# Transposing one of two expert tiles on VectorE instead of TensorE in a fused conditional-mixing and mixture-of-LoRA kernel

## What is computed

```python
# x: (128, 64, 1024) f32, cond_128: (128, 128)
h = gelu(embedding @ W0 + b0); h = gelu(h @ W1 + b1)
att = softmax(h @ W2 + b2)                              # (128, 8)
agg_w = einsum('bk,koi->boi', att, weight[..., 0])      # a 64x64 channel mix for each sample
agg_b = att @ bias_k
y = einsum('boi,bih->boh', agg_w, x) + agg_b[:, :, None]
y = y.reshape(-1, 1024)                                 # 8192 rows
probs = softmax(y @ W_router.T)                         # 8 experts
topk_probs, topk_idx = top_k(probs, 2); topk_probs /= sum(topk_probs)
combine = the two weights put at their experts          # (8192, 8)
h = einsum('nd,erd->ner', y, A)                         # 8 experts x rank 16 = 128 columns
hw = h * combine[:, :, None]                            # the weighted activations
out = x + y @ W_base.T + b_base + einsum('ner,eor->no', hw, B) * 2
```

## Time and profile before

| | before |
|---|---|
| median of 3 runs | 954.34 us (954.16 to 954.8) |
| the profiled execution, its own time | 954.3 us |
| its span, first to last instruction | 952.6 us |
| granted TensorE clock | 1.00 in all 40 slices |
| PE busy | 945.1 us (99%) |
| DVE busy | 695.5 us (73%) |
| ACT busy | 332.8 us (35%) |
| POOL busy | 89.1 us (9%) |
| HBM traffic over the span | 117 GB/s |

### The profile page before, as it was taken

The page is one execution under the profiler, slowest core; times in us unless marked ns, Lnnn a source line. Parts: engine busy times, 40 slices in busy tenths (PEclk is TensorE's granted clock), DMA queues, the critical chain, the costliest instruction groups (busy, mean ns, idle before and its releaser), DMA issues.

```text
span 952.6 us, 18810 instructions
## 1 busy us (share of the span) xinstructions
PE 945.1 (99%) x6745; PEld 940.2 (99%) x6745; DVE 695.5 (73%) x1554; ACT 332.8 (35%) x671; POOL 89.1 (9%) x134
## 2 busy tenths in 40 slices
PE   9999999999999999999999999999999999999997
PEld 8999999999999999999999999999999999999997
DVE  4889776768776768777777777777777677767686
ACT  5653332333332333332333333333333333323431
POOL 0011010101010100100100100010101010101010
PEclk9999999999999999999999999999999999999999
DMA  8434444343444354435353434344434344444434
GB/s 304 140 75 132 110 119 132 92 132 91 111 115 133 90 134 91 111 113 130 94 133 92 112 113 119 105 118 105 114 113 109 115 108 104 120 118 104 120 90 111
DMA packets 35233, 111.33 MB, mean 117 GB/s; under 512 B 13040, under 2 KB 13424, under 8 KB 30864
## 3 DMA queue, kind: packets, MB, share of 16 engines
q1 hardware_dynamic: 25712, 76.36, 21.9%
q0 software_dynamic: 9216, 33.56, 21.2%
q10 hardware_dynamic: 288, 1.19, 0.4%
HBM read 75.37 MB, written 35.65 MB: 117 GB/s over the span
## 4 chain that ended last, share of the span: by engine, by line
PE 97%; DMA 1%; DVE 1%; issue 0%; ACT 0%; DVEq 0%; ACTq 0%
PE ps L416 25%; PE ps L420 25%; PE ps L418 25%; PE ps L476 9%; PE ps L452 4%; PE ps L450 4%; PE ps L454 4%; DMA w_stage<-in_wide 1%; PE ps L499 1%; PE ps L442 0%; PE ps L443 0%; PE ps L502 0%; PE ps L513 0%; DVE sum L931 0%; DVE x_sb L1220 0%
## 5 line engine op out<-in xcount | busy, mean ns | idle before, releaser
L416 PE MATMUL ps<-w_hi,x_hi 128*128 128x290 f32 x1544 | 460.3, 298 | 0.3 <-DVE sum L931 0.3
L418 PE MATMUL ps<-w_lo,x_hi 128*128 128x290 f32 x1544 | 457.7, 296 | 0.0
L420 PE MATMUL ps<-w_hi,x_lo 128*128 128x290 f32 x1544 | 456.9, 296 | 0.0
L416 PEld LDWEIGHTS ps<-w_hi,x_hi 128*128 128x128 f32 x1544 | 291.5, 189 | 2.5 <-issue 1.5
L420 PEld LDWEIGHTS ps<-w_hi,x_lo 128*128 128x128 f32 x1544 | 291.3, 189 | 0.0
L418 PEld LDWEIGHTS ps<-w_lo,x_hi 128*128 128x128 f32 x1544 | 291.2, 189 | 0.0
L684 ACT CAST x_hi<-xT_sb 128x512 fp32r<-128x512 f32 x186 | 115.6, 621 | 190.9 <-DVE xT_sb L928 163.4
L912 DVE TENSOR_TENSOR x_lo<-xT_sb,x_hi 128x512 fp32r<-128x512 f32 x186 | 127.4, 686 | 34.3 <-ACT x_hi L684 34.3
L889 POOL DMA_DIRECT2D x_sb<-in_x x64 | 56.4, 881 | 512.0 <-DVE x_sb L1002 512.0
L988 DVE TENSOR_TENSOR hwT_lo<-ps,hwT_hi 128x128 fp32r<-128x128 f32 x64 | 18.7, 291 | 97.7 <-ACT hwT_hi L696 96.9
L699 ACT COPY sum<-ps 128x580 f32<-128x580 f32 x96 | 61.9, 645 | 62.9 <-PE ps L420 62.1
(11 more groups left out here) (123 smaller groups left out, 1127.6 us busy)
## 6 DMA issues: line engine op xcount, KB each, us to landing
x_sb<-in_x POOLq DMA_DIRECT2D x64, 512.0 KB, 5.4
result<-x_sb SPq DMA_DIRECT2D x63, 512.0 KB, 2.8
xT_sb<-in_xT SPq DMA_DIRECT2D x31, 1024.0 KB, 4.8
b_sb<-in_wide SPq DMA_DIRECT2D x2, 1160.0 KB, 14.7
agg_w_rows<-agg_w SPq DMA_DIRECT2D x1, 2048.0 KB, 7.5
mix<-agg_w_rows SPq DMA_DIRECT2D x124, 16.0 KB, 2.5
w_stage<-in_wide ACTq DMA_DIRECT2D x2, 580.0 KB, 8.0
w_stage<-in_wide SPq DMA_DIRECT2D x2, 580.0 KB, 11.5
```

Source lines behind the costliest of these rows:

```text
L416: nc.tensor.matmul(dst, x_hi[:, s, rows], high[:, c, cols], start=first, stop=False, skip_group_check=True)
L418: nc.tensor.matmul(dst, x_hi[:, s, rows], low[:, c, cols], start=False, stop=False, skip_group_check=True)
L420: mm = nc.tensor.matmul(dst, x_lo[:, s, rows], high[:, c, cols], start=False, stop=last, skip_group_check=True)
```

## The change

In units 2 to 30 the transpose of the lower tile's hw (tiles 1 to 29 by unit) is taken off TensorE. VectorE does it in 16 STREAM_TRANSPOSE instructions of 32x32, from hw to a new SBUF tile lower_hwT, block (i, j) to block (j, i). Each raises a semaphore, and ScalarE waits for all 16. For this VectorE's route of the lower tile is moved up, ahead of the low part of A22's x (x_low(u, "A22")), and the 16 transposes follow it, also ahead of x_low(u, "A22"). hwT_hi and hwT_lo are then made from lower_hwT in SBUF rather than from PSUM. Unit 1 and the last unit keep TensorE's transpose for both tiles, and so does every unit for its upper tile; the waits of ScalarE for TensorE's transposes are renumbered for it.

```diff
@@ -173,6 +175,7 @@
         bias_out = sb("bias_out", [P, D])
         ar = sb("ar", [P, AR])
         hw = sb("hw", [P, ER])
+        lower_hwT = sb("lower_hwT", [P, P])
         hwT_hi = sb("hwT_hi", [P, P], F32R)
         hwT_lo = sb("hwT_lo", [P, P], F32R)
 
@@ -244,6 +247,7 @@
         ratio_done = sem("ratio_done")
         hw_done = sem("hw_done")
         hwT_mm = sem("hwT_mm")
+        lower_hwT_made = sem("lower_hwT_made")
         hwT_hi_done = sem("hwT_hi_done")
         hwT_lo_done = sem("hwT_lo_done")
         out_mm = sem("out_mm")
@@ -610,7 +614,8 @@
                     pe.wait_ge(w_lo_done, SPLIT_AT["T3"])
                 pe.wait_ge(x_lo_done, splits(u, "S3"))
                 product_part(a, "S3", 0, False)
-                transpose_hw(u - 1, 1)
+                if first:
+                    transpose_hw(u - 1, 1)
                 product_part(a, "S3", 1, False).then_inc(product_mm, 1)
                 experts(u - 1, 1)
                 pe.wait_ge(p5_saved, u)
@@ -691,9 +696,16 @@
                 act.wait_ge(routed, tile_no(u, side) * ROUTE_STEPS + 4)
                 nc.scalar.activation(ratio[:], top_gap[:], ACT.Exp).then_inc(ratio_done, 1)
 
-            def hwT_high(u, side):
-                act.wait_ge(hwT_mm, tile_no(u, side) + 1)
+            def hwT_high(transposes):
+
+                act.wait_ge(hwT_mm, transposes)
                 nc.scalar.copy(hwT_hi[:], hwT).then_inc(hwT_hi_done, 1)
+
+            def lower_hwT_high(u):
+
+                act.wait_ge(lower_hwT_made, u * (BLOCKS * BLOCKS))
+                act.wait_ge(out_mm, tile_no(u, 1))
+                nc.scalar.copy(hwT_hi[:], lower_hwT[:]).then_inc(hwT_hi_done, 1)
 
             def save(dst, first, done):
                 nc.scalar.copy(dst[:], acc(first)).then_inc(done, 1)
@@ -807,7 +819,7 @@
                 act.wait_ge(product_mm, products(u, "A11"))
                 save(sum1, a, p1_saved)
                 x_high("S3")
-                hwT_high(u - 1, 0)
+                hwT_high(1 if first else u + 1)
                 if first:
                     act.wait_ge(t_made, T_AT["T3"])
                     split_weight(T3, t_stage)
@@ -824,7 +836,10 @@
                 gate(u - 1, 1)
                 act.wait_ge(product_mm, products(u, "S1"))
                 save(sum3, b, p5_saved)
-                hwT_high(u - 1, 1)
+                if first:
+                    hwT_high(2)
+                else:
+                    lower_hwT_high(u - 1)
                 z11_high(u)
                 act.wait_ge(xT_in, u * 16 + 16)
                 act.wait_ge(product_mm, products(u, "S3"))
@@ -846,7 +861,7 @@
             act.wait_ge(product_mm, last_products("A11"))
             save(sum1, a, p1_saved)
             x_high("S3")
-            hwT_high(u - 1, 0)
+            hwT_high(LAST + 1)
             act.wait_ge(s_made, sums(u, "S4"))
             act.wait_ge(product_mm, last_products("A12"))
             x_high("S4")
@@ -857,20 +872,20 @@
             mix_high(u, 1)
             gate(u - 1, 1)
             z11_high(u)
-            hwT_high(u - 1, 1)
+            hwT_high(LAST + 2)
             act.wait_ge(product_mm, last_products("S3"))
             save(sum3, a, p5_saved)
             act.wait_ge(product_mm, last_products("A22"))
             nc.scalar.copy(last_hi_left, acc(a)).then_inc(z21_hi_done, 1)
             gate(u, 0)
-            hwT_high(u, 0)
+            hwT_high(LAST + 3)
             act.wait_ge(z22_summed, u + 1)
             nc.scalar.copy(last_hi_right, sum3[:]).then_inc(z22_hi_done, 1)
             for part in range(2):
                 act.wait_ge(last_half_summed, part + 1)
                 nc.scalar.copy(z_hi_right[:, part, :], sum2[:, part, :]).then_inc(last_half_hi_done, 1)
             gate(u, 1)
-            hwT_high(u, 1)
+            hwT_high(LAST + 4)
 
         @block.gpsimd
         def _(pool):
@@ -983,9 +998,17 @@
                     ar[:, lora].rearrange("p (e r) -> p e r", e=EXPERTS), first_w[:, 0:1],
                     expert_w[:].unsqueeze(2).to_broadcast([P, EXPERTS, RANK]), ALU.mult, ALU.mult).then_inc(hw_done, 1)
 
-            def hwT_low(u, side):
+            def transpose_lower(u):
+
+                dve.wait_ge(hw_done, tile_no(u, 1) + 1)
+                for i in range(BLOCKS):
+                    for j in range(BLOCKS):
+                        there, here = slice(j * BLOCK, (j + 1) * BLOCK), slice(i * BLOCK, (i + 1) * BLOCK)
+                        nc.vector.transpose(lower_hwT[there, here], hw[here, there]).then_inc(lower_hwT_made, 1)
+
+            def hwT_low(u, side, whole=hwT):
                 dve.wait_ge(hwT_hi_done, tile_no(u, side) + 1)
-                nc.vector.tensor_tensor(hwT_lo[:], hwT, hwT_hi[:].bitcast(F32), ALU.subtract).then_inc(hwT_lo_done, 1)
+                nc.vector.tensor_tensor(hwT_lo[:], whole, hwT_hi[:].bitcast(F32), ALU.subtract).then_inc(hwT_lo_done, 1)
 
             def result(u, side):
                 t = tile_no(u, side)
@@ -1134,9 +1157,10 @@
                 dve.wait_ge(x_lo_done, splits(u, "A12"))
                 make_s4(u)
                 x_low(u, "S4")
+                route(u - 1, 1)
+                transpose_lower(u - 1)
                 x_low(u, "A22")
-                route(u - 1, 1)
-                hwT_low(u - 1, 1)
+                hwT_low(u - 1, 1, lower_hwT[:])
                 dve.wait_ge(stored[0], u * 16)
                 z11_low(u)
                 put_biases(u, 0)
```

More of the change, by code:

```diff
@@ L80 @@
 GROUPS, GROUP_ROWS = 4, 32
+BLOCK, BLOCKS = 32, 4
 GROUP_COLS = CH * CH // GROUPS
```

## The result

The changed kernel takes 969.32 us (median of 5 runs, 968.18 to 969.53) against 954.58 us before on the same chip: a ratio of 1.0154, 95% interval 1.0142 to 1.0165. It is slower by 1.5%, and the forecast of 951.1 us was wrong in size and in sign. The profiled execution has a span of 967.7 us where before had 952.6, at a clock of 0.999.

A forecast was written before the change was run, and what follows sets the result against it. The prediction took TensorE as the bound, holding 97% of the chain. Only the removed transposes counted, with VectorE's blocks and the move at nothing: 954.34 - 3.28 = 951.06, forecast 951.1 us, range 950.5 to 952.7.

The forecast's parts named there:

- The price of a block: On VectorE, each 32x32 transpose was taken at 0.12 us, from the starts of small steps L973 to L976.
- What it adds on VectorE: VectorE's 16 blocks cost 1.9 us a unit, bounds 0 and 4.6 us, mostly in its idle time before hwT_lo.
- What is moved later: x_low of A22 ends 3.6 us later, delaying SP's xT load; 1.65 us remain before TensorE notices, so no cost.
- The removed transposes: On TensorE, 29 lower-tile transposes at 0.113 us each between matmul starts save 3.28 us, all on the chain.
- rival 1: Blocks from 0.22 us each make xT late and stop PE at mix_upper's z12_lo; 983 us at 0.29 us; chance 6%.
- The upper bound of 0.29 us: Highest price per VectorE block, from the 128-column subtraction L988 if nothing overlaps.
- The threshold: Blocks may cost 0.22 us each before the late xT load, via make_s1 and z12_low, stops TensorE.
- The move costed at nothing: Delaying x_low of A22 on VectorE, and so SP's xT load, was priced at zero, covered by 1.65 us of slack.
- Rival 2: Late xT load pushes the x load and SP's store, delaying make_s2 and upper hw; 954.3 to 970 us; chance 7%.
- Rivals 3 and 4: On TensorE, half the transpose gain stays (952.7 us, chance 4%), or the whole 0.272 us duration returns (946.4 us, chance 1%).
- the credit: The 3.28 us that TensorE was to win from 29 removed transposes.

The follow-up runs named there:

- dose runs: The change with 8, 14 or 20 blocks per loop unit instead of 16 (unit 2 keeps at least 16): 952.51, 955.77 and 997.22 us.
- the version with x_low of A22 between: The change with x_low of A22 placed between the lower tile's route and the 16 blocks instead of behind them: 954.93 us.
- the version with z11 ahead: The change with x_low of A22 between route and blocks, and z11's parts made before hwT_hi and hwT_lo: 951.78 us, 951.61 us when repeated.

## Why the prediction was wrong

Two terms failed. The price of a block in "What it adds on VectorE" was put at 0.12 us, and 0.234 us were measured. The cover in "What is moved later", behind which I costed the move at nothing, was put at 1.65 us beyond those 1.9 us of blocks; the runs show 1.2 us (3.1 less 1.9). The first error alone would have turned the sign, by some 2 us; with the second it became 15. The mechanism of the result was foreseen, with its place: make_s1 late for xT, z12_low late, PE's wait in mix_upper. It had 6%.

- *The removed transposes, 3.28 us*: right. Without blocks 3.2 us were measured, and the loop's unit is 28.61 us, as forecast.
- *The price of a block, 0.12 us*: wrong, 0.234 us. I took the distance between two starts of small steps, which overlap; the transposes don't. It was also one of the short distances: in the same timeline the route's steps start 0.07 to 0.27 us apart, and behind the first one, of only 8 columns, it is 0.25 us (524.64 to 524.89). So the argument against rival 1, that only instructions of 128 columns and more are as dear as 0.22 us, misread the rows. For 16 that is 1.8 us more than the sum had, a unit. The upper bound of 0.29 us held it.
- *The threshold, 0.22 us*: too high. The dose runs put the knee at 13.4 blocks of 0.234 us, 3.1 us in all, which is 0.196 us for each of 16. Of the 0.4 us between, 0.17 us are the weight load: I counted slack up to the matmul of mix_upper's second piece at 510.42, but the wait stands ahead of its weight load, which in the kernel before starts at 510.25. Another 0.11 us are the gain itself: without the lower transpose TensorE comes to that weight load sooner, 15.92 us behind the start of x_low of S4 in the kernel without blocks, where it is 16.03 in the kernel before (medians). hw started 0.1 us later than worked out. From issue to make_s1 it took 4.87 us in the median of the changed units (4.96 in the one shown), where I had used the median landing of 4.8. These add up to the 0.4 us within the reading. make_s1 may thus start some 0.6 us late before TensorE notices (z12_low ends 0.8 us ahead of the weight load in the kernel before, less the 0.11, and less 0.06 from its end to the weight load), so the 0.28 us above would be hidden.
- *So the sum*: TensorE lost 0.59 us a unit (29.2 less 28.61), 17 us in 29 units, and 1.4 more in the one long unit, against a gain of 3.3. By my own threshold the measured price would have made 3.75 less 3.57 us (1.92 of blocks and 1.65 of slack), 0.18 us a unit, some 5 us; the other 12 come from the overrated slack.
- *The move costed at nothing*: right alone, 954.89 us; but it spent part of the slack that the blocks then needed. I priced it with that cover named and took the cover as given.
- *Rival 2*, the other transfers pushed: not seen in the change. Its chain, from a store over make_s2 to the upper hw, costs time in the version with x_low of A22 between, but because VectorE lets the store go later, not because the load of xT pushes it.
- *Rivals 3 and 4*: both fell with the kernel without blocks.
- *The skill's rules*: the Trainium skill (VectorE: DVE Perf Modes, Rules for kernel authors) leaves a 128x128 transpose to TensorE. The change as made bears it out, and the version with z11 ahead does not: 16 blocks are worth it where they fall into idle time. The prediction took the fixed cost of 58 cycles from the Trainium skill (VectorE: DVE Perf Modes, the section on the TRN2 errata), 94 ns a block by my estimate. The row of the trace, 0.203 us, is over twice that. The same section of the Trainium skill says right under its table that the row with the 58 comes out too low and that the measured fixed term is about 150 cycles, which by estimate makes 190 ns a block; the prediction left that out.

A chance of 6% for a rival whose threshold (0.22) lay between my value and my own upper bound (0.29) was too small. The range was drawn around the credit, which was known to a tenth of a microsecond, and not around the unseen price.

## What to carry to other kernels

When a step is moved behind new work, find the queue that waits for it, here SP's load into a single buffer, and follow that wait round to the bound engine before pricing anything; a thing that costs nothing alone may have spent the slack. Count slack up to the weight load and not to the matmul, take off what the change itself wins for the engine that waits, and take the price of an instruction that the trace doesn't have at its full duration, since only rows of the same kind, with the same operands and partitions, show whether it overlaps. If idle time is to carry work, order the queue so that what others wait for leaves first, and fill the wait for a partner engine with work that doesn't need it.

## What the runs showed of the hardware

- A STREAM_TRANSPOSE of 32x32 f32 between SBUF tiles lasts 0.203 us, and 16 in a row with a signal each, each to other partitions than the one before, start 0.234 us apart; with one signal 0.218 us. One of 128x128 lasts 0.311 us.
- A 128x128 f32 transpose on TensorE between matmuls costs 0.11 us of its time (3.2 us for 29), where its row shows 0.27 us.
- One load of xT took 6.2 us to land instead of 4.8, and that unit was 1.4 us longer than its neighbours, since the slack was gone. The same load was slow in three more kernels whose load goes out late (6.1 to 6.3 us) and took 4.8 us in the kernel before. In the kernel that holds the load until z11_low is done, the loads took 5.1 us in the median. The kernel before kept to 28.71 to 28.73 us in every unit from the third on.
